# Attention outputs turned in 32x32 blocks on VectorE instead of whole on TensorE, in a decoder layer kernel

## Chip, cores and metric

The kernel runs on one core of a Trainium2 chip. The metric is the device time of one execution in microseconds (us). The kernel before takes 2980.4 us, the median of three runs (2975.87 to 2981.51).

## The reference

One decoder layer in float32 over `x` of 128 sequences x 128 tokens x 256: self attention, cross attention to `ctx` of the same shape, and a feed-forward part, each with layer norm ahead and a residual behind. 16 heads of 16 channels. Cut to what matters:

```python
def attn(xn, kv, mask):                     # self: kv = xn, no mask
    Q, K, V = proj(xn, Wq, bq), proj(kv, Wk, bk), proj(kv, Wv, bv)
    scores = einsum('bhqd,bhkd->bhqk', Q, K) / sqrt(16)
    if mask is not None:
        scores = where(mask == 0, 1e-9, scores)      # cross only
    out = einsum('bhqk,bhkd->bhqd', softmax(scores), V)
    return out.transpose(0, 2, 1, 3).reshape(B, S, 256) @ Wo.T + bo
x = x + attn(layernorm(x), layernorm(x), None)
x = x + attn(layernorm(x), ctx, mask)
x = x + ffn(layernorm(x))     # ternary weights, 256 -> 1024, gelu, layer norm, 1024 -> 256
```

Masked keys keep a weight of exp(1e-9 - max): they count in the softmax.

## The kernel before

There are three blocks of the program. `setup` turns and splits weights and builds masks, `attention` does both attentions, `ffn` the rest from a scratch tensor in HBM. The change is in `setup` (one constant) and `attention`.

`attention` works on groups of 4 sequences (G = 4, T = 512 tokens, 32 groups). Two chains of buffers exist, `self` and `cross`, each with four PSUM banks `self_bk`, `cross_bk`. The order is written out by hand, for each engine its own (`pe_slot`, `dve_slot`, `act_slot`, `pool_slot`, `sp_slot`), with semaphores between them. A `step` has two slots, and the engines run steps in a loop:

```python
        def step(slot, i):
            slot(crs, slf, present(i - 1), present(i), present(i + 1), present(i))
            slot(slf, crs, present(i + 1), present(i - 1), present(i), present(i + 2))
```

The arguments are y, x, att, tail, proj, norm. In a slot chain y does its attention core (scores, softmax, values of group att) while chain x ends another group (tail: divide, output projection), projects queries, keys and values of a third (proj), and y's next input is normalised (norm). The first slot, y = cross, is called the cross turn below, the second, y = self, the self turn. `proj` and `tail` work of x fills TensorE's time between scores.

The attention core. `pe_scores` (L802) computes scores of one sequence and eight heads, VectorE takes the maxima (`dve_max`, L651), TensorE waits for those of two steps before. The negated maxima are transposed by TensorE (L890), copied out by ScalarE (L604, `negmT`) and written by four DMAs into rows of `stk`. `pe_shifted` (L820) computes transposed, shifted scores; cross adds masks (L785). ScalarE exponentiates them (L630), and `pe_values` (L831) multiplies by the values, four heads into one bank of 128 partitions, 32 partitions (16 channels, a sum, padding) a head: four such sets, qd = 0 to 3, are called strips here. So the outputs have channels on partitions and queries on columns.

What happens to a strip: it is copied from PSUM into `oT`, a view of the `qk` buffer (VectorE L747 for qd 0 to 2, ScalarE L633 for qd 3); `pe_turn_outputs` (L838) turns it with four float32 transposes, so that queries lie on partitions; `dve_normalise` adds the masked sums in cross (L667), takes the reciprocal of the sums (L671) and multiplies (L673) into `att`. The last strip is handled at the head of the next slot, after the first maxima. `att` is split into two float16 parts (ScalarE L565, GpSimd L501), turned by TensorE (`turn_att`, L777), copied out by ScalarE (`both`, L549) into `ahl` and multiplied by the output weights (`products`, L766). ScalarE scales the product (L582), GpSimd adds the residual (L516), and in the cross turn VectorE normalises that for cross (`cross_xn`, L741).

The masked part of cross: `earg` from the negated maxima (L711), its exponential `ew` (L600), the sums of the masked values by TensorE (L949), both multiplied on VectorE into `ue` (L717, L720).

Queries and keys reach `stk` by DMA: SyncE issues 24 transfers a chain and group (`stack_rows`, L467) once ScalarE has written the four projection tiles (L540), the later ones also after VectorE's low parts (L644). The first scores of the chain wait for all 24.

Queue order that matters: ScalarE has `ew`, then `negmT`, then four DMA issues, then `products_out` (L582); GpSimd has the residual, its copy, `rstd` and the splits in that order; VectorE has `cross_xn` ahead of the strips of the cross turn.

## Time and profile before

| | |
|---|---|
| median of 3 runs | 2980.4 us |
| profiled execution, its own time | 2975.84 us |
| its span | 2973.8 us |
| granted TensorE clock, mean | 0.963 |
| busy: TensorE, VectorE, ScalarE, GpSimd | 2587.0, 2044.6, 1793.0, 977.4 us |
| attention loop | from about 88 to about 2330 us |

The page gives shares of the whole span, which has three stages with different limits. "Start" and "us" in a timeline are the start and length of a run of equal instructions; a bracket names the idle time before it on its engine and what ended it. PE is TensorE's matmuls, PEld its weight loads, DVE VectorE, ACT ScalarE, POOL GpSimd, SP SyncE. Float32 matmuls show as two records each.

### The profile page before, as it was taken

Reading aid. Unit: us, or ns where it says so; the run is one execution under the profiler, and the core shown is the slowest. Engines: PE = TensorE matmul, PEld = TensorE weight load, DVE = VectorE, ACT = ScalarE, POOL = GpSimd, SP = SyncE. Lnnn points to the kernel's source line nnn. Section 1 sums busy time; section 2 is a strip of 40 time slices with the busy share of each in tenths; the row PEclk is TensorE's granted clock in tenths of the full one; section 3 lists DMA queues with packets and bytes.
Section 4 is the critical chain, followed back from the end, with each engine's and each line's share of the span. In section 5 each row is a group of like instructions: output and inputs, shape, how many; then the busy total and the mean of one; then the engine's idle time right before and its main releaser. Section 6 shows DMA issues by size and latency. Waiting matters only on the chain. (4 is left out here: it accounts for less than half of the span.)

```text
span 2973.8 us, 79195 instructions
## 1 busy us (share of the span) xinstructions
PE 2587.0 (87%) x31607; PEld 1762.5 (59%) x31607; DVE 2044.6 (69%) x4066; ACT 1793.0 (60%) x2350; POOL 977.4 (33%) x630
## 2 busy tenths in 40 slices
PE   3478889898888998898998889998888499999999
PEld 2245556555555555555555555565555267777777
DVE  4256676776667666767766676667775288888887
ACT  1245665665665656656656656556665277777776
POOL 2223333333333333333333333333332133333432
PEclk7689999999999999999999999999999799999999
DMA  2133433333333334333333333333332211111111
GB/s 75 32 62 76 83 80 84 71 71 80 79 83 73 71 74 82 80 86 71 71 76 81 80 78 71 72 81 80 85 67 40 50 58 56 56 56 56 56 57 43
DMA packets 186380, 206.83 MB, mean 70 GB/s; under 512 B 35152, under 2 KB 136912, under 8 KB 186320
## 3 DMA queue, kind: packets, MB, share of 16 engines
q1 hardware_dynamic: 163056, 186.77, 27.0%
q10 hardware_dynamic: 23264, 19.22, 4.3%
q8 instruction: 43, 0.70, 0.1%
q14 instruction: 17, 0.14, 0.0%
HBM read 54.87 MB, written 33.55 MB: 30 GB/s over the span
## 5 line engine op out<-in xcount | busy, mean ns | idle before, releaser
L651 DVE TENSOR_REDUCE self_mx<-self_bk 128x8 f32<-128x1024 f32 x256 | 306.4, 1215 | 47.4 <-PE self_bk L802 47.2
L651 DVE TENSOR_REDUCE cross_mx<-cross_bk 128x8 f32<-128x1024 f32 x256 | 303.4, 1216 | 43.5 <-PE cross_bk L802 43.3
L630 ACT ACTIVATE prob<-cross_bk 128x1024 f32<-128x1024 f32 x256 | 248.3, 1022 | 75.6 <-PE cross_bk L820 75.2
L1244 PE MATMUL hbk<-wfcT,ffn_xhl 128*128 128x512 f16 x1024 | 263.8, 381 | 0.0
L1212 PE MATMUL ybk<-wpT,ghl 128*128 128x256 f16 x2048 | 260.2, 273 | 0.8 <-DVE ffn_y L1176 0.7
L630 ACT ACTIVATE prob<-self_bk 128x1024 f32<-128x1024 f32 x256 | 246.4, 1054 | 6.8 <-PE self_bk L820 6.6
L516 POOL TENSOR_TENSOR cross_src<-self_att,self_xb 128x1024 f32<-128x1024 f32 x32 | 75.4, 2356 | 532.6 <-ACT self_att L582 532.6
L1191 DVE SCALAR_TENSOR_TENSOR ghl<-tbk,lnwc,ghl 128x512 f16<-128x512 f32 x256 | 189.0, 739 | 73.7 <-ACT ghl L1120 72.0
L1212 PEld LDWEIGHTS ybk<-wpT,ghl 128*128 128x128 f16 x2048 | 200.1, 98 | 63.8 <-DVE ghl L1191 0.9
L1120 ACT ACTIVATE ghl<-tbk,lnwc 128x512 f16<-128x512 f32 x256 | 174.7, 683 | 75.4 <-PE tbk L1226 75.4
L747 DVE COPY self_qk<-cross_bk 128x512 f32<-128x512 f32 x96 | 66.4, 692 | 204.0 <-PE cross_bk L831 204.0
L1126 ACT ACTIVATE hid<-hbk 128x512 f32<-128x512 f32 x256 | 152.9, 597 | 64.1 <-PE hbk L1244 56.7
L758 PE MATMUL self_bk<-self_xhl,WT 128*128 128x512 f16 x768 | 188.8, 383 | 3.0 <-ACT self_xhl L549 2.0
L785 PE MATMUL cross_bk<-maskB,pick 64*128 64x512 bf16 x1024 | 158.0, 387 | 37.0 <-DMA cross_stk<-cross_qk 23.3
L497 POOL TENSOR_TENSOR self_rstd<-self_ve,mhalf 128x4 f32<-128x4 f32 x32 | 32.2, 1007 | 459.3 <-DVE self_ve L737 459.3
L1152 DVE BATCH_NORM_STATS2 hstats<-hid 128x6 f32<-128x512 f32 x256 | 173.9, 679 | 1.1 <-ACT hid L1126 0.8
L820 PE MATMUL self_bk<-self_stk 64*128 64x128 f16 x2048 | 96.9, 220 | 88.9 <-ACT prob L630 59.7
L785 PE MATMUL cross_bk<-maskBT,pick 64*128 64x512 bf16 x1024 | 157.0, 386 | 13.5 <-ACT prob L630 8.5
L540 ACT ACTIVATE self_qk<-self_bk,bcol 128x512 f16<-128x512 f32 x128 | 87.9, 686 | 126.6 <-PE self_bk L758 126.5
L1226 PE MATMUL tbk<-ident,hid 128*128 128x128 f32 x1024 | 153.5, 273 | 0.8 <-ACT hid L1126 0.8
L644 DVE SCALAR_TENSOR_TENSOR self_qk<-self_bk,bcol,self_qk 128x512 f16<-128x512 f32 x128 | 92.9, 745 | 85.9 <-ACT self_qk L540 85.9
L720 DVE TENSOR_TENSOR ue<-cross_bk,ew 128x512 f32<-128x512 f32 x64 | 44.3, 692 | 149.2 <-PE cross_bk L949 149.2
(200 smaller groups left out, 6068.7 us busy)
## 6 DMA issues: line engine op xcount, KB each, us to landing
self_stk<-self_qk SPq DMA_DIRECT2D x768, 64.0 KB, 2.3
cross_stk<-cross_qk SPq DMA_DIRECT2D x768, 64.0 KB, 2.3
self_src<-in_x SPq DMA_DIRECT2D x32, 512.0 KB, 3.9
ctx_in<-in_ctx SPq DMA_DIRECT2D x32, 512.0 KB, 4.8
x_scratch<-cross_att SPq DMA_DIRECT2D x32, 512.0 KB, 3.0
ffn_src<-x_scratch SPq DMA_DIRECT2D x32, 512.0 KB, 3.8
out<-ffn_y SPq DMA_DIRECT2D x32, 512.0 KB, 2.9
self_stk<-self_negmT ACTq DMA_DIRECT2D x128, 64.0 KB, 2.6
```

Source lines behind the costliest of these rows:

```text
L630: act.activation(y.prob[:, qd % 2, two:two + 2], y.bk[:, two:two + 2, :], ACT.Exp, scale=EXP_SCALE).then_inc(y.exp_done, 1)
L651: dve.tensor_reduce(ch.mx[:, 8 * m:8 * m + 8].rearrange("p (j r) -> p r j", r=2), ch.bk[:, o:o + 2, :].rearrange("p r (j k) -> p r j k", j ...
L758: last = nc.tensor.matmul(ch.bk[:, bank, :], sh.WT[:, w, wp, kt, tile * P:(tile + 1) * P], moving[:, a, kt, :], start=(n == 0 and kt == 0) ...
L785: pe.matmul(ch.bk[:, bank + r, :], sh.pick[rows, h], mask[rows, h], start=(h == 0), stop=False, skip_group_check=True)
L820: last = pe.matmul(ch.bk[:, bank + r, b * S:(b + 1) * S], ch.stk[rows, 1, p % 4, p // 4, b * S:(b + 1) * S], ch.stk[rows, 0, p % 4, p // 4 ...
L1120: act.activation(ghl[:, HI, s], tbk[:, TURN_BANK[s]], ACT.Copy, scale=sh.lnwc[:, s:s + 1]).then_inc(ghi_ready, 1)
L1126: act.activation(hid[:, half, s // 2, s % 2 * HF:(s % 2 + 1) * HF], hbk[:, s % 2], ACT.Gelu).then_inc(hid_ready, 1)
L1152: dve.bn_stats(hstats[:, s // 2, s % 2], hid[:, half, s // 2, s % 2 * HF:(s % 2 + 1) * HF]).then_inc(hstats_done, 1)
L1191: dve.scalar_tensor_tensor(ghl[:, LO, s], tbk[:, TURN_BANK[s]], sh.lnwc[:, s:s + 1], ghl[:, HI, s], ALU.mult, ALU.subtract).then_inc(glo_r ...
L1212: last = pe.matmul(ybk[:, b], ghl[:, part, t, b * S:(b + 1) * S], sh.wpT[:, t], start=(t == 0 and part == HI and b % 2 == 0), stop=(t == F ...
L1226: last = pe.transpose(tbk[:, TURN_BANK[s], b * S:(b + 1) * S], hid[:, 1 - half, b, s * P:(s + 1) * P], sh.ident[:, :])
L1244: last = pe.matmul(hbk[:, s % 2], xhl[:, half, part, kt, s // 2 * S:(s // 2 + 1) * S], sh.wfcT[:, kt, s % 2 * HF:(s % 2 + 1) * HF], start= ...
```

## The change

VectorE transposes each strip in 32x32 blocks, PSUM to PSUM, as soon as its values are there (`dve_turn_outputs`, all four strips). After that, partitions hold 32 queries of a block for each of four heads, columns hold block and channel. It divides in this layout, writes `att` so that two strips stand side by side in each 32 columns, and transposes `att` back in 32x32 blocks into `attT` (`dve_turn_att`, SBUF to SBUF, two halves): channels on partitions again, as the output projection needs them. ScalarE and GpSimd split `attT` into `ahl` directly. `pe_turn_outputs`, `turn_att`, the copies into `oT` and the copies into `ahl` are gone. The heads are dealt anew to strips (`stack_rows`, `pe_values`). The masked sums, their counts and exponentials are built in the same layout: 16 small matmuls turn the negated maxima (`m_turned`), L949 becomes 16 matmuls of 32 columns, and setup writes a count per block (`cntL`). In the core:

```diff
+        def dve_turn_outputs(dve, ch, g, qd):
+            dve.wait_ge(ch.pv_done, 4 * g + qd + 1)
+            dve.transpose(turned_bank(ch, qd), out_bank(ch, qd)).then_inc(ch.o_turned, 1)
         def dve_normalise(dve, ch, g, qd):
-            dve.wait_ge(ch.oT_ready, 4 * g + qd + 1)
-            o = turned_bank(ch, qd).rearrange("p (b h c) -> p b h c", b=G, h=4)[:, :, :, 0:HD + 1]
+            dve.wait_ge(ch.o_turned, 4 * g + qd + 1)
+            o = turned_bank(ch, qd).rearrange("p (b t c) -> p b t c", b=G, t=BLOCKS)[:, :, :, 0:HD + 1]
...
-                dve.tensor_tensor(total[:, qd], o, ue[:, :, 4 * qd:4 * qd + 4, :], ALU.add).then_inc(ch.den_ready, 1)
+                dve.tensor_tensor(o, o, ue[:, :, :, qd, :].rearrange("p t b c -> p b t c"), ALU.add).then_inc(ch.den_ready, 1)
...
+        def dve_turn_att(dve, ch, g, kt):
+            dve.wait_ge(ch.ao_ready, 4 * g + 2 * kt + 2)
+            wait(dve, ch.a_lo, 2 * (g - 1) + kt + 1)
+            dve.transpose(ch.attT[:, kt], ch.att[:, :, :].rearrange("p b d -> p (b d)")[:, kt * T:(kt + 1) * T]).then_inc(ch.aT_ready, 1)
...
+            if tail is not None:
+                dve_turn_outputs(dve, x, tail, QUADS - 1)
             maxima(0)
             if tail is not None:
                 dve_normalise(dve, x, tail, QUADS - 1)
+                dve_turn_att(dve, x, tail, 1)
             maxima(1, 2, 3)
...
-                    dve.wait_ge(y.negm_ready, att + 1)
-                    dve.tensor_scalar(earg[:, :], y.negm[:, :], 0.0, MASKED * HD ** 0.5, ALU.min, ALU.add).then_inc(earg_ready, 1)
+                    dve.wait_ge(m_turned, att + 1)
+                    dve.tensor_scalar(earg[:, :], y.bk[:, 1, 0:BLOCKS * G * QUADS], 0.0, MASKED * HD ** 0.5, ALU.min, ALU.add).then_inc(earg_ready, 1)
...
                 for qd in range(QUADS - 1):
-                    dve.wait_ge(y.pv_done, 4 * att + qd + 1)
-                    dve.tensor_copy(y.oT[:, qd], out_bank(y, qd)).then_inc(y.o_out, 1)
-                    if qd:
-                        dve_normalise(dve, y, att, qd - 1)
-                dve_normalise(dve, y, att, QUADS - 2)
+                    dve_turn_outputs(dve, y, att, qd)
+                    dve_normalise(dve, y, att, qd)
+                    if qd == 1:
+                        dve_turn_att(dve, y, att, 0)
...
-        def pe_turn_outputs(pe, ch, g, qd):
-            pe.wait_ge(ch.o_out, 4 * g + qd + 1)
-            for b in range(G):
-                last = pe.transpose(turned_bank(ch, qd)[:, b * S:(b + 1) * S], ch.oT[:, qd, b * S:(b + 1) * S], sh.ident[:, :])
-            last.then_inc(ch.oT_ready, 1)
...
-            def turn_att():
-                if tail is not None:
-                    pe.wait_ge(x.as_lo, 2 * tail + 2)
-                    turn_split(x, x.tb, x.asp).then_inc(x.aT_ready, 1)
...
+                    if y.cross:
+                        for jq in range(4):
+                            for block in range(BLOCKS):
+                                at = block * G * QUADS
+                                last = pe.matmul(y.bk[VW * jq:VW * (jq + 1), 1, at:at + G * QUADS], sh.ident16[:, VW * block:VW * (block + 1)],
+                                                 y.negm[:, :].rearrange("p (a j) -> p j a", j=4)[:, jq], start=True, stop=True, skip_group_check=True)
+                        last.then_inc(m_turned, 1)
...
-                for b in range(G):
-                    last = pe.matmul(y.bk[:, 2 + b // 2, (b % 2) * D:(b % 2 + 1) * D], sh.maskcT[:, :],
-                                     y.vals[:, b, :, 0:HD], start=True, stop=True)
-                    if b % 2:
+                for block in range(BLOCKS):
+                    for jq in range(4):
+                        heads = y.vals[:, :, :, 0:HD].rearrange("p b (k j s) d -> p j (b k) s d", k=KT, s=2)[:, jq]
+                        at = (block % 2) * D
+                        last = pe.matmul(y.bk[VW * jq:VW * (jq + 1), 2 + block // 2, at:at + D], sh.maskcT[:, VW * block:VW * (block + 1)],
+                                         heads, start=True, stop=True, skip_group_check=True)
+                    if block % 2:
                         last.then_inc(u_mm, 1)
+                pe.wait_ge(earg_ready, att + 1)
```

ScalarE's and GpSimd's side, and setup:

```diff
-            def split_outputs(ch, g, quads, cols):
+            def split_outputs(ch, g, kt):
                 if g is not None:
-                    act.wait_ge(ch.ao_ready, 4 * g + quads)
-                    act.activation(ch.asp[:, HI, :, cols], ch.att[:, :, cols], ACT.Copy).then_inc(ch.as_hi, 1)
+                    act.wait_ge(ch.aT_ready, 2 * g + kt + 1)
+                    act.activation(ch.ahl[:, HI, kt], ch.attT[:, kt], ACT.Copy).then_inc(ch.a_hi, 1)
...
-                both(x.aT_ready, x.ahl, x.tb, x.ahl_ready, tail)
...
-                act.wait_ge(y.pv_done, 4 * att + QUADS)
-                act.wait_ge(y.o_out, 4 * att + QUADS - 1)
-                act.activation(y.oT[:, QUADS - 1], out_bank(y, QUADS - 1), ACT.Copy).then_inc(y.o_out, 1)
...
+                for jq in range(4):
+                    for block in range(BLOCKS):
+                        nc.vector.tensor_scalar(cntL[VW * jq:VW * (jq + 1), block:block + 1], cntW[VW * block:VW * (block + 1), :], WS, None,
+                                                ALU.mult).then_inc(cnt_done, 1)
```

How rows move. First VectorE at the seam of a cross and a self turn, from the third strip of a cross group (names as in the text above; `cross_bk<-cross_bk` and `self_bk<-self_bk` with STREAM_TRANSPOSE are the turned strips). Before:

```order
L667 TENSOR_TENSOR total<-self_bk,ue 128x272 [waits cross_oT_ready]
L671 RECIPROCAL cross_rec<-total 128x16 [waits cross_den_ready]
L673 TENSOR_TENSOR cross_att<-total,cross_rec 128x4x64 [waits cross_rec_ready]
L651 TENSOR_REDUCE self_mx<-self_bk 128x2x4 [waits self_s_mm]
L667 TENSOR_TENSOR total<-cross_bk,ue 128x272 [waits cross_oT_ready]
L671 RECIPROCAL cross_rec<-total 128x16 [waits cross_den_ready]
L673 TENSOR_TENSOR cross_att<-total,cross_rec 128x4x64 [waits cross_rec_ready]
L651 TENSOR_REDUCE self_mx<-self_bk 128x2x4 [waits self_s_mm] x3
```

With the change:

```order
L682 STREAM_TRANSPOSE cross_attT<-cross_att 128x512 [waits cross_ao_ready]
L651 STREAM_TRANSPOSE self_bk<-self_bk 128x512 [waits cross_pv_done]
L666 TENSOR_TENSOR self_bk<-self_bk,ue 128x16x17 [waits cross_o_turned]
L670 RECIPROCAL cross_rec<-self_bk 128x16 [waits cross_den_ready]
L674 TENSOR_TENSOR cross_att<-self_bk,cross_rec 128x16x16 [waits cross_rec_ready]
L651 STREAM_TRANSPOSE cross_bk<-cross_bk 128x512 [waits cross_pv_done]
L644 TENSOR_REDUCE self_mx<-self_bk 128x2x4 [waits self_s_mm]
L666 TENSOR_TENSOR cross_bk<-cross_bk,ue 128x16x17 [waits cross_o_turned]
L670 RECIPROCAL cross_rec<-cross_bk 128x16 [waits cross_den_ready]
L674 TENSOR_TENSOR cross_att<-cross_bk,cross_rec 128x16x16 [waits cross_rec_ready]
L682 STREAM_TRANSPOSE cross_attT<-cross_att 128x512 [waits cross_ao_ready]
L644 TENSOR_REDUCE self_mx<-self_bk 128x2x4 [waits self_s_mm] x3
```

Four transposes stand in this stretch that did not: one ahead of the third strip's addition (a copy stood earlier), one ahead of the first maxima, and one each for the halves of `att`; the second one of these stands ahead of the second maxima.

TensorE at the same seam, from the last shifted scores of the cross turn. Before:

```order
L831 MATMUL self_bk<-prob,cross_vals 32x128 x16
L838 MATMUL self_bk<-ident,cross_qk 128x128 x4
L831 MATMUL cross_bk<-prob,cross_vals 32x128 x16
L838 MATMUL self_bk<-ident,cross_qk 128x128 x4
L802 MATMUL self_bk<-self_stk 128x128 x8
L838 MATMUL cross_bk<-ident,cross_qk 128x128 x4
L777 MATMUL cross_bk<-ident,cross_xs 128x128 x16
L802 MATMUL self_bk<-self_stk 128x128 x16
L777 MATMUL cross_bk<-ident,ctx_s 128x128 x16
L802 MATMUL self_bk<-self_stk 128x128 x8
```

With the change:

```order
L845 MATMUL self_bk<-prob,cross_vals 32x128 x16
L845 MATMUL cross_bk<-prob,cross_vals 32x128 x16
L816 MATMUL self_bk<-self_stk 128x128 x8
L791 MATMUL cross_bk<-ident,cross_xs 128x128 x16
L816 MATMUL self_bk<-self_stk 128x128 x16
L791 MATMUL cross_bk<-ident,ctx_s 128x128 x16
L816 MATMUL self_bk<-self_stk 128x128 x8
```

The three turns of strips are gone; the rest keeps its order.

TensorE in the cross turn, from the output products to the masked sums. Before:

```order
L766 MATMUL self_bk<-WT,self_ahl 128x256 x12
L890 MATMUL cross_bk<-ident,cross_negm 16x128 x4
L766 MATMUL self_bk<-WT,self_ahl 128x256 x12
L766 MATMUL self_bk<-WT,self_xhl 128x256 x24
L949 MATMUL cross_bk<-cross_vals,maskcT 128x256 x4
```

With the change:

```order
L780 MATMUL self_bk<-WT,self_ahl 128x256 x12
L893 MATMUL cross_bk<-ident,cross_negm 16x128 x4
L899 MATMUL cross_bk<-cross_negm,ident 32x16 x16
L780 MATMUL self_bk<-WT,self_ahl 128x256 x12
L780 MATMUL self_bk<-WT,self_xhl 128x256 x24
L957 MATMUL cross_bk<-cross_vals,maskcT 32x256 x16
```

Sixteen small matmuls are new behind the transposes of the negated maxima, and the masked sums are cut into sixteen.

## Rows read from the trace of the kernel before

**Rows 1.** The page's busy times, shares and instruction counts.
```profile
PE 2587.0 (87%) x31607; PEld 1762.5 (59%) x31607; DVE 2044.6 (69%) x4066; ACT 1793.0 (60%) x2350; POOL 977.4 (33%) x630
```

**Rows 2.** The tile maskcT: durations in ns, first and last start in us.
```profile
L949 PE MATMUL cross_bk<-cross_vals,maskcT x256: 379/379/634, 226.2 to 2332.2; 128*128 128x256 f32 x128
```

**Rows 3.** Timeline of VectorE: start us, length us, instruction, idle time before.
```profile
1126.43 1.27 DVE L747 COPY cross_qk<-self_bk 128x512 f32<-128x512 f32 x2
...
1130.93 0.43 DVE L667 TENSOR_TENSOR total<-self_bk,ue 128x272 f32<-128x272 f32 x1
1131.39 0.25 DVE L671 RECIPROCAL cross_rec<-total 128x16 f32<-128x16 f32 x1
1131.68 0.42 DVE L673 TENSOR_TENSOR cross_att<-total,cross_rec 128x256 f32<-128x256 f32 x1
...
1136.45 2.34 DVE L651 TENSOR_REDUCE self_mx<-self_bk 128x8 f32<-128x1024 f32 x2
...
1195.28 1.27 DVE L747 COPY cross_qk<-self_bk 128x512 f32<-128x512 f32 x2
```

**Rows 4.** Timeline of TensorE in the same group.
```profile
1127.17 0.66 PE L838 MATMUL self_bk<-ident,cross_qk 128*128 128x128 f32 x4 [1.67 <-DVE cross_qk L747]
...
1136.68 1.87 PE L777 MATMUL cross_bk<-ident,ctx_s 128*128 128x128 f16 x16 [1.43 <-DVE cross_att L673]
...
1139.02 1.95 PE L758 MATMUL cross_bk<-cross_xhl,WT 128*128 128x512 f16 x6
...
1145.58 1.47 PE L758 MATMUL cross_bk<-ctx_hl,WT 128*128 128x512 f16 x6
...
1165.26 0.61 PE L785 MATMUL cross_bk<-maskB,pick 64*128 64x512 bf16 x4 [0.29 <-DMA cross_stk<-cross_qk]
```

**Rows 5.** Timeline of TensorE in the next group.
```profile
1206.90 1.47 PE L758 MATMUL cross_bk<-cross_xhl,WT 128*128 128x512 f16 x6
...
1212.99 1.47 PE L758 MATMUL cross_bk<-ctx_hl,WT 128*128 128x512 f16 x6
```

**Rows 6.** Windows: busy us of each engine, PEclk, DMA share, GB/s.
```profile
1132.40:1136.60 4.20, 2.57 (x45) 2.00 (x44) 3.99 (x8) 2.84 (x4) 1.64 (x1) 1.00 0.00 0
1136.60:1139.00 2.40, 2.32 (x24) 1.98 (x24) 2.19 (x2) 0.80 (x2) 0.67 (x1) 0.50 0.00 0
```

**Rows 7.** Timeline of SyncE's queue: start, length of the issues.
```profile
1147.80 15.52 SPq L467 DMA_DIRECT2D cross_stk<-cross_qk  x24
...
1215.21 15.50 SPq L467 DMA_DIRECT2D cross_stk<-cross_qk  x24
...
1284.08 15.52 SPq L467 DMA_DIRECT2D cross_stk<-cross_qk  x24
```

**Rows 8.** Instructions grouped by line and shape: busy us, mean ns, idle before.
```profile
L831 PE MATMUL self_bk<-prob,cross_vals 128*32 128x128 f32 x3072 | 104.7, 277 | 0.0
L673 DVE TENSOR_TENSOR cross_att<-total,cross_rec 128x256 f32<-128x256 f32 x128 | 100.6, 786 | 4.4
L747 DVE COPY self_qk<-cross_bk 128x512 f32<-128x512 f32 x96 | 66.4, 692 | 204.0 <-PE cross_bk L831 204.0
L838 PE MATMUL self_bk<-ident,cross_qk 128*128 128x128 f32 x384 | 63.4, 288 | 52.9 <-DVE cross_qk L747 52.9
L949 PE MATMUL cross_bk<-cross_vals,maskcT 128*128 128x256 f32 x256 | 61.4, 383 | 0.0
L777 PE MATMUL cross_bk<-ident,cross_asp 128*128 128x128 f16 x512 | 35.0, 223 | 3.7 <-POOL cross_asp L501 3.7
L890 PE MATMUL cross_bk<-ident,cross_negm 128*16 128x128 f16 x128 | 12.5, 220 | 2.0 <-DVE cross_negm L709 2.0
```

**Rows 9.** Timeline of ScalarE in the cross turn.
```profile
1112.84 0.59 ACT L604 ACTIVATE cross_negmT<-cross_bk 16x512 f16<-16x512 f16 x1 [0.93 <-PE cross_bk L890]
...
1116.06 1.02 ACT L582 ACTIVATE self_att<-self_bk 128x1024 f32<-128x1024 f32 x1 [2.63 <-issue]
```

**Rows 10.** Timeline of VectorE in setup.
```profile
53.23 0.14 DVE L257 TENSOR_SCALAR cntW<-cntW 128x1 f32<-128x1 f32 x1
```

More of the change, by code:

```diff
@@ L31 @@
 VW = 32
+BLOCKS = S // VW
 WS = 8.0
@@ L77, in __init__ @@
         self.maskcT = sb("maskcT", [P, S])
-        self.cntW = sb("cntW", [P, 1])
+        self.cntL = sb("cntL", [P, BLOCKS])
         self.mfloor = sb("mfloor", [P, 1])
@@ L343, in __init__ @@
         self.prob = prob
-        self.oT = self.qk[:, :, :, :].rearrange("p a k t -> p (a k t)").bitcast(F32).rearrange("p (q t) -> p q t", q=QUADS)
         self.mx = sb(n + "_mx", [P, G * H])
@@ L350, in __init__ @@
         self.att = sb(n + "_att", [P, G, D])
-        self.asp = sb(n + "_asp", [P, 2, G, D], F16)
+        self.attT = sb(n + "_attT", [P, KT, T])
         self.ahl = sb(n + "_ahl", [P, 2, KT, T], F16)
@@ L381, in __init__ @@
         self.pv_done = sem(n + "_pv_done")
-        self.o_out = sem(n + "_o_out")
-        self.oT_ready = sem(n + "_oT_ready")
+        self.o_turned = sem(n + "_o_turned")
         if self.cross:
@@ L387, in __init__ @@
         self.ao_ready = sem(n + "_ao_ready")
-        self.as_hi = sem(n + "_as_hi")
-        self.as_lo = sem(n + "_as_lo")
         self.aT_ready = sem(n + "_aT_ready")
-        self.ahl_ready = sem(n + "_ahl_ready")
+        self.a_hi = sem(n + "_a_hi")
+        self.a_lo = sem(n + "_a_lo")
         self.op_mm = sem(n + "_op_mm")
@@ L416, in attention @@
         chl = sb("ctx_hl", [P, 2, KT, T], F16)
-        earg = sb("earg", [P, G * H])
-        ew = sb("ew", [P, G, H])
-        ue = sb("ue", [P, G, H, HD + 1])
-        total = sb("total", [P, QUADS, G, 4, HD + 1])
+        earg = sb("earg", [P, BLOCKS * G * QUADS])
+        ew = sb("ew", [P, BLOCKS, G, QUADS])
+        ue = sb("ue", [P, BLOCKS, G, QUADS, HD + 1])
         held = sb("held_wait", [P, 1])
@@ L449, in out_bank @@
         def out_bank(ch, qd):
-            return ch.bk[:, 2, :] if qd == QUADS - 1 else (slf if ch.cross else crs).bk[:, 2 + qd % 2, :]
+            return ch.bk[:, ch.tb, :] if qd == QUADS - 1 else (slf if ch.cross else crs).bk[:, 2 + qd % 2, :]
         def turned_bank(ch, qd):
-            return ch.bk[:, 1, :] if qd == QUADS - 1 else (slf if ch.cross else crs).bk[:, (0, 1, 3)[qd], :]
+            return ch.bk[:, ch.tb + 1, :] if qd == QUADS - 1 else (slf if ch.cross else crs).bk[:, (0, 1, 3)[qd], :]
         def stack_rows(sp, ch, g, block, heads):
@@ L465, in stack_rows @@
             for j in heads:
-                rows, to = slice(HD * j, HD * j + HD), HALF * (j % 2) + HD * block
-                sp.dma_start(ch.stk[to:to + HD, :, j // 2], ch.qk[rows, parts]).then_inc(ch.stacked, 16)
+                rows, to = slice(HD * j, HD * j + HD), HALF * (j // 2 % 2) + HD * block
+                sp.dma_start(ch.stk[to:to + HD, :, 2 * (j % 2) + j // 4], ch.qk[rows, parts]).then_inc(ch.stacked, 16)
         def sp_slot(sp, y, x, att, tail, proj, norm):
@@ L497, in deviations, with lo @@
                     nc.gpsimd.tensor_tensor(y.rstd[:, :], y.ve[:, :], sh.mhalf[:, :], ALU.pow).then_inc(y.rstd_ready, 1)
-            def lo(src, split, hi_ready, lo_ready, count, cols=slice(0, D)):
+            def lo(src, split, hi_ready, lo_ready, count):
                 pool.wait_ge(hi_ready, count)
-                nc.gpsimd.tensor_tensor(split[:, LO, :, cols], src[:, :, cols], split[:, HI, :, cols],
-                                        ALU.subtract).then_inc(lo_ready, 1)
+                nc.gpsimd.tensor_tensor(split[:, LO], src, split[:, HI], ALU.subtract).then_inc(lo_ready, 1)
             if tail is not None:
-                lo(x.att, x.asp, x.as_hi, x.as_lo, 2 * tail + 2, LAST)
+                lo(x.attT[:, 1], x.ahl[:, :, 1], x.a_hi, x.a_lo, 2 * tail + 2)
             if x.cross:
@@ L586, in act_slot @@
                 both(x.xT_ready, x.xhl, x.pb, x.xhl_ready, proj)
-                split_outputs(x, tail, 4, LAST)
+                split_outputs(x, tail, 1)
                 both(cT_ready, chl, x.tb, chl_ready, proj)
-                tiles(0, 1)
-                both(x.aT_ready, x.ahl, x.tb, x.ahl_ready, tail)
-                tiles(2, 3)
+                tiles(0, 1, 2, 3)
             else:
-                split_outputs(x, tail, 4, LAST)
+                split_outputs(x, tail, 1)
                 both(x.xT_ready, x.xhl, x.pb, x.xhl_ready, proj)
-                both(x.aT_ready, x.ahl, x.tb, x.ahl_ready, tail)
                 tiles(0, 1, 2, 3)
```

54 lines of the change are left out of this document (25 added, 29 removed).

## Prediction

> **What bounds the kernel now.** I read the page's busy shares first: TensorE is busy 87% of the span, VectorE 69% [rows 1]. Read alone, that says that matmul time removed is time gained. It is an average, so I took one group of the attention loop apart. The masked-sum matmuls of L949 come once a group, first at 226.2 and last at 2332.2 us [rows 2]: 31 distances of 67.9 us. A group has two halves: the cross turn (cross attention of one group beside the self projections) and the self turn (the reverse).
>
> In the timelines I looked for the wait that ends last in each half. Three pieces make up a group:
>
> *Piece 1, from the end of cross_xn on VectorE to the last projection tile of the self turn.* VectorE copies the first outputs from 1126.43, then adds, inverts and multiplies four strips while it also owes TensorE the first maxima; it hardly rests until 1138.8 [rows 3]. TensorE waits for it 1.67 us for a copy and 1.43 us for cross_att, then runs at half speed: the first tile takes 1.95 us instead of 1.47 in the next group [rows 4, 5]. The windows show the granted clock at 1.00 up to 1136.6 and 0.50 (1.2 GHz) after it; before the fall the engine had been busy 2.57 us of 4.2 [rows 6]. The last tile starts at 1145.58 and ends about 1.4 later, near 1147.0: piece 1 is 20.5 us. In the next group, at full clock, it is 19.1 (1195.28 to 1212.99 + 1.4) [rows 3, 5].
>
> *Piece 2, from that tile to the first cross scores.* SyncE issues 24 transfers of cross_qk in 15.5 us, from 1147.80, and the scores at 1165.26 end on one of them [rows 4, 7]. That is 18.2 us, whatever TensorE does meanwhile.
>
> *Piece 3, from those scores through projections, negated maxima, masked sums, residual and normalisation back to the end of cross_xn:* the rest, about 30.1 us, in which VectorE's maxima, TensorE and the ScalarE-GpSimd path of the residual take turns.
>
> The starts of the 24 transfers are 67.41 us apart around the full-clock group and 68.87 around another [rows 7].
>
> **The change part by part.**
>
> *Removed from TensorE.* Per group eight turns of four float32 transposes (L838): 63.4 us for 96 of them is 0.66 each, about 0.59 up to the next start, so 4.7 us; and two 16-transpose turns of the split outputs (L777), 35.0 us for 32, 1.09 each and about 0.9 net, so 1.8 us [rows 8]. ScalarE loses two wide copies and two narrow ones; neither piece 1 nor piece 2 waits for them, TensorE's tiles run meanwhile, so they count nothing (if it were short there, it would gain more). Three of the eight turns lie in piece 2: they count nothing, since the scores wait for the transfers. If the transfers were shorter, they would be worth 1.8 us.
>
> *Moved to VectorE.* In each half three copies (0.69 us, PSUM to SBUF) become 32x32 transposes, PSUM to PSUM, a fourth replaces ScalarE's copy, and two more turn the divided outputs. No 32x32 transpose is in the trace. From below I bound one by the 272-column addition, 0.43 us, from above by one maxima operation over 1024 columns, 1.17 (2.34 for two) [rows 3]. I take the copy's 0.69 [rows 8]: the same 512 columns and type, the same engine, a PSUM source. The Trainium skill has 311 ns for a transpose of 128 columns of bf16 (VectorE: DVE Perf Modes, The three transpose paths) and one element a cycle in that mode (Vector Engine (DVE) Microarchitecture Reference, 3.8); from these pages I estimate 0.71 us, which would move the sum by under 0.2 us a group, and no row here shows it.
>
> *Division.* The multiply in cross takes 0.79 us in the mean, but 0.42 where nothing disturbs it [rows 3, 8]. After the change its numerator comes from PSUM, as the self one's always does, and I take 0.42 for all.
>
> *Piece 1 after.* From the end of cross_xn VectorE is one chain. A strip is transpose 0.73 (0.69 and a semaphore), addition 0.46, reciprocal 0.29 and multiply 0.35 (0.42 less the overlap of an independent next one), by the distances in [rows 3]: 1.83. Two strips 3.7, turn of the first half 0.69, third strip 1.8: 6.2. Fourth transpose 0.6: 6.8. First maxima 1.15: 7.9. Addition, reciprocal, multiply of the fourth strip 1.2: 9.1. Turn 0.69: 9.8. Second maxima 1.15: 11.0. TensorE's fourth scores (0.3) and then the first tile wait for those second maxima, so the tile starts at 11.3; before it was 11.6 at full clock (1206.90 - 1195.28) [rows 3, 5]. The other tiles and scores need 6.6 us, 0.9 less than before, since the turn between them is gone. Piece 1 is 17.9: 1.2 saved. If the clock falls as before, the turn of ctx_s starts at 9.1 and takes 1.9, scores 0.6, the tile 1.95 [rows 4], the rest 5.2: 18.7, 1.8 saved against 20.5. So of the 3.3 us of turns and 3.1 us of waits that disappear from TensorE here, VectorE's chain hands most back: the wait for a copy becomes a wait for a transpose and a division.
>
> *Piece 3 after.* Gone are one L838 turn and the self turn of split outputs, 1.5 us. But VectorE now has the turn of the second half (0.69) ahead of the second maxima, and the next scores wait for those: walking it, the last self tile ends 0.3 us earlier than now. Then 16 small matmuls (32 weight columns, 16 moving columns) follow the negated maxima; the exponent's argument, ScalarE's exponential and, behind it, ScalarE's copy of the negated maxima wait for them. That copy (1112.84) stands ahead of four DMA issues, the output copy at 1116.06 [rows 9], GpSimd's residual and the next cross_xn: all of that moves. From below the matmuls cost 0.5 us together (L831: 104.7 us for 3072 halves, 0.03 each), from above 1.3 (L890: 12.5 us for 128, 0.10 less the overlap, 0.08 each) [rows 8]. I take 0.5, as these too write strips of 32; but four in a row write the same strip, which keeps the upper end open. With 0.25 for the argument, 0.1 net for the exponential ahead of the copy, and 0.3 off for the earlier tile, piece 3 grows by 0.55, at the upper end by 1.35. The masked sums become 16 matmuls to strips of 32 instead of 4 to 128 columns, now 61.4/32 = 1.9 us [rows 8]. L831 runs its four strips side by side (16 matmuls with 128 columns in 1.09, where four with 256 to full width need 1.9), so I leave them at 1.9; one after another they would be 7.
>
> *Sum.* Full-clock group: -1.2 + 0.55 = -0.65, 66.8. Low-clock group: -1.8 + 0.55 = -1.25, 67.6. The mean of 67.9 says that now about a third of the groups pay for the low clock. Afterwards TensorE waits four times 0.8 to 1.4 us around little work in piece 1, so I let two thirds pay: 67.3, or 0.65 to 0.7 less, times 31 = -21. The last group's turns, with no other work as cover, give 3 to 4 us. Setup, which everything waits for, has 15 more tiny VectorE operations like the one of 0.14 us [rows 10], half of it up to the next start: +1. In all -24. The profiled execution took 2975.8 (span 2973.8), so it would be 2952; the runs' median is 4.6 above it. Against that median: 2980.4 - 24 = 2956, its own range 2938 to 2974. A measurement of this kernel can tell about 0.2%, 6 us, from no change.
>
> TensorE's clock fell after a stretch in which transposes and waits alternated [rows 6]. The Trainium skill (TensorE: Matmul & The Clock Gate, PE-mode transpose) says that transposes don't count as activity like matmuls; by that rule taking them away can't bring the clock down, the share of low groups stays at a third, and the sum is -29, 2951.
>
> **The rivals.**
>
> *TensorE is the bound after all: 2788, chance 0.05.* 6.5 us less 0.5, times 32. For it: 87% busy. Against it: piece 2 ends on a transfer, piece 1 on VectorE.
>
> *Transposes are cheap: 2910, chance 0.10.* At 0.43 six of them on piece 1's chain save another 1.5 us a group: -46. For it: the engine does no arithmetic in them; against: nor does it in a copy.
>
> *Small matmuls one after another: 2980, chance 0.08.* 1.3 us instead of 0.5 is +0.8 a group, and the gain is gone.
>
> *The clock, slower: 3010, chance 0.12.* TensorE gets thinner exactly where it waits. If every group has a low stretch in piece 1 and a second one in piece 3 (where it will wait about 1 us just before the cross scores), each is 67.6 + 1.46 = 69.0: +1.1 x 31 = +33, less 3. It decides once every second group has the added stretch. For it: the clock fell after a 1.43 us wait. Against: it didn't after 1.67 us [rows 4, 6].
>
> *Transposes are dear: 3012 to 3056, chance 0.10.* At 1.0 us six on the chain cost 1.8 more a group, at 1.17 2.9; with piece 3's one or two +34 to +78 over no change. Gain and loss meet at about 0.80 us. Masked sums one strip after another would be worse still (+5 a group) and are in this chance.
>
> That the change doesn't do what it says is ruled out by the rows of the order: the turns are gone.
>
> **How the numbers follow.** Forecast 0.55, the rivals 0.05, 0.10, 0.08, 0.12, 0.10. The range 2908 to 3015 takes in cheap transposes, small matmuls and the clock; the first rival and most of the last, about 0.13, stay outside. Faster: the forecast less a margin, and 0.15: 0.68. Within 0.2%: 0.10. Slower: 0.22.
>
> **What would show it.** Right: 24 transfers again in 15.5 us and the cross scores ending on them, now after about 1 us of wait; VectorE without a gap from cross_xn to the third maxima, transposes at 0.65 to 0.75; TensorE's busy share down to some 81% with a span down by 1%; groups 67.3 apart. Wrong: cross scores that don't wait for a transfer, a transpose off 0.69 by over 0.1, small matmuls over 1 us, a clock below 1.00 in piece 3.

## The result, and the profile after

| | before | after |
|---|---|---|
| median | 2978.25 us (4 runs) | **3103.61 us** (4 runs, 3102.15 to 3113.85) |
| profiled execution / span | 2975.84 / 2973.8 us | 3104.04 / 3101.9 us |
| mean granted clock | 0.963 | 0.912 |

The ratio is 1.0428, 95% interval 1.0402 to 1.0453: 4.3% slower, where I forecast 0.8% faster (2956) and gave 3015 as the upper end. Ratios here and below leave out runs more than 1.5% above the fastest of their kernel; medians take in all of them. The page of the kernel after, busy times beside [rows 1], then its clock in 40 slices, then its instruction queue:

```profile
PE 2518.3 (81%) x30839; PEld 1644.6 (53%) x30839; DVE 2148.8 (69%) x4273; ACT 1636.0 (53%) x2222; POOL 975.3 (31%) x630
...
PEclk7689898899999899999999999999899889999999
...
q8 instruction: 285, 4.67, 0.6%
```

TensorE's busy time fell by 69 us, VectorE's rose by 104. The line that matters is the last: q8 moves instructions, in packets of 16 KB, and there are 285 of them. The page of the kernel before has 43:

```profile
q8 instruction: 43, 0.70, 0.1%
```

For the stretch from 400 to 2200 us, inside the attention loop, the views of the DMA queues say (packets, MB, share), first before, then after:

```profile
q8 instruction: 2, 0.03, 0.0%
```

```profile
q8 instruction: 222, 3.64, 0.9%
```

A group takes 72.8 us now, so this is 9 packets a group: the loop's instructions are fetched anew in every pass. The kernel before fetched none from 340.3 to 2189.0 us.

The sizes of single instructions held, but for the small matmuls, which took less. Instructions of the kernel after, grouped by line and shape (they answer to [rows 8]):

```profile
L651 DVE STREAM_TRANSPOSE cross_bk<-cross_bk 128x512 f32<-128x512 f32 x128 | 93.1, 727 | 147.4 <-PE cross_bk L845 147.4
L957 PE MATMUL cross_bk<-cross_vals,maskcT 128*32 128x256 f32 x1024 | 63.3, 389 | 0.0
L682 DVE STREAM_TRANSPOSE cross_attT<-cross_att 128x512 f32<-128x512 f32 x64 | 45.5, 711 | 7.9 <-DVE cross_att L674 0.2
L899 PE MATMUL cross_bk<-cross_negm,ident 128*32 128x16 f16 x512 | 9.5, 177 | 0.0
```

A 32x32 transpose of 512 columns takes 0.73 us (0.71 from SBUF) where I took 0.69; the masked sums take 63.3 us for 61.4; the 16 small matmuls 9.5/32 = 0.30 a group, for 0.5.

Where the time went, in one group. SyncE's queue, beside [rows 7]:

```profile
1061.84 18.34 SPq L469 DMA_DIRECT2D cross_stk<-cross_qk  x24
...
1135.39 17.37 SPq L469 DMA_DIRECT2D cross_stk<-cross_qk  x24
1152.98 1.32 SPq L488 DMA_DIRECT2D x_scratch<-cross_att  x1
...
1208.71 17.04 SPq L469 DMA_DIRECT2D cross_stk<-cross_qk  x24
```

TensorE, beside [rows 4]:

```profile
1150.78 1.08 PE L845 MATMUL self_bk<-prob,self_vals 128*32 128x128 f32 x32 [0.42 <-ACT prob L626]
1155.82 1.03 PE L799 MATMUL cross_bk<-maskB,pick 64*128 64x512 bf16 x4 [3.96 <-DMA cross_stk<-cross_qk]
```

The 24 issues take 17.0 to 18.3 us for 15.5, the scores come 20.4 us after the first of them for 17.5, after a wait of 3.96 us, and then TensorE runs at half clock: masks of 1.03 us for 0.61.

For the comparisons below I cut a group at four events: S1 from SyncE's first issue of cross_stk to the first cross scores, S2 to the masked sums, S3 to the end of cross_xn, S4 to the next first issue. (Piece 2 is S1 and the 0.8 us ahead of it, piece 3 is S2 and S3, piece 1 is S4 less 0.8.) Means over the middle 19 groups, us; "packets" is q8 of the whole run; "low" is the time at 1.2 GHz in one group, also a mean over these 19:

| kernel | median | S1 | S2 | S3 | S4 | group | packets | low |
|---|---|---|---|---|---|---|---|---|
| before | 2978.25 | 17.44 | 20.16 | 9.95 | 20.71 | 68.26 | 43 | 2.0 |
| after | 3103.61 | 20.24 | 21.05 | 10.49 | 20.99 | 72.76 | 285 | 12.4 |
| after_pad90 | 2997.60 | 17.47 | 20.31 | 10.29 | 21.06 | 69.14 | 43 | 6.8 |
| after_pad30 | 3128.08 | 20.12 | 22.79 | 10.29 | 20.58 | 73.78 | 285 | 14.2 |
| before_pad60 | 3098.24 | 20.71 | 21.59 | 9.94 | 20.57 | 72.81 | 286 | 6.1 |
| before_pad128 | 2976.60 | 17.44 | 20.16 | 9.94 | 20.72 | 68.26 | 44 | 2.0 |
| after_pad70_fill | 2946.56 | 17.48 | 20.39 | 10.29 | 19.23 | 67.39 | 43 | 0.5 |
| before_pad116_fill | 2948.02 | 17.46 | 20.16 | 9.95 | 19.85 | 67.42 | 44 | 0.0 |
| after_pad90_late | 2944.16 | 17.46 | 20.09 | 10.29 | 19.51 | 67.35 | 43 | 5.0 |
| after_pad90_twice | 3047.29 | 17.49 | 20.31 | 10.29 | 22.49 | 70.57 | 43 | 9.0 |
| after_late | 3062.71 | 20.65 | 21.23 | 10.57 | 19.03 | 71.48 | 285 | 10.6 |
| after_pad70_late_fill | **2914.49** | 17.39 | 20.09 | 10.29 | 18.46 | 66.23 | 43 | 0.4 |

### The profile page after: what moved, and what is told of

The parts are those of the page before. It is cut to its first block and busy times, and to the rows that moved or that the text cites. A ratio compares the mean times of both kernels' runs of the same rounds, so it can differ in the third digit from the quotient of the medians.

```text
span 3101.9 us, 77805 instructions
## 1 busy us (share of the span) xinstructions
PE 2518.3 (81%) x30839; PEld 1644.6 (53%) x30839; DVE 2148.8 (69%) x4273; ACT 1636.0 (53%) x2222; POOL 975.3 (31%) x630
## 5 line engine op out<-in xcount | busy, mean ns | idle before, releaser
L644 DVE TENSOR_REDUCE self_mx<-self_bk 128x8 f32<-128x1024 f32 x256 | 299.8, 1207 | 24.5 <-PE self_bk L816 23.7
L799 PE MATMUL cross_bk<-maskB,pick 64*128 64x512 bf16 x1024 | 193.3, 461 | 139.7 <-DMA cross_stk<-cross_qk 122.4
L816 PE MATMUL self_bk<-self_stk 48*128 48x128 f16 x2048 | 117.6, 244 | 108.0 <-DVE self_mx L644 50.6
L651 DVE STREAM_TRANSPOSE cross_bk<-cross_bk 128x512 f32<-128x512 f32 x128 | 93.1, 727 | 147.4 <-PE cross_bk L845 147.4
L564 ACT ACTIVATE self_ahl<-self_attT 128x512 f16<-128x512 f32 x64 | 42.5, 665 | 261.0 <-DVE self_attT L682 261.0
L816 PEld LDWEIGHTS self_bk<-self_stk 48*128 48x128 f16 x2048 | 67.1, 104 | 199.9 <-DVE self_mx L644 71.8
L539 ACT ACTIVATE cross_qk<-cross_bk,bcol 128x512 f16<-128x512 f32 x128 | 87.9, 687 | 159.5 <-PE cross_bk L772 159.5
```

The source lines that it names most:

```text
L539: act.activation(ch.qk[:, 1 + n // 2, n % 2], qk_bank(ch, n), ACT.Identity, bias=sh.bcol[:, 2 * ch.which + n // 2, n % 2:n % 2 + 1]).then_ ...
L644: dve.tensor_reduce(ch.mx[:, 8 * m:8 * m + 8].rearrange("p (j r) -> p r j", r=2), ch.bk[:, o:o + 2, :].rearrange("p r (j k) -> p r j k", j ...
L799: pe.matmul(ch.bk[:, bank + r, :], sh.pick[rows, h], mask[rows, h], start=(h == 0), stop=False, skip_group_check=True)
L816: last = pe.matmul(ch.bk[:, 2 * (m % 2) + r, j * S:(j + 1) * S], ch.stk[rows, 0, j, eight, b * S:(b + 1) * S], ch.stk[rows, 1, j, eight, b ...
```

## The experiments

Theory A: most of the loss is instruction loading, decided by where the loop's body happens to lie on the packets. Theory B, its rival: the chain of transposes on VectorE and the clock. For what A leaves over, two more: C, the clock, and D, VectorE's chain.

### Moving the loop by tiny matmuls

One edit in four doses: N matmuls of 16 columns, two instructions each, ahead of TensorE's attention loop. Nothing waits for them.

```diff
+                for _ in range(N):
+                    pe.matmul(slf.bk[:, 3, 0:16], sh.ident16[:, :], sh.ident16[:, 0:16], start=True, stop=True, skip_group_check=True)
                 steps(pe, pe_slot)
```

The changed kernel, N = 90:

> The changed kernel with 90 tiny matmuls (a weight load and a matmul each, 180 TensorE instructions, some 10 us in all at most) ahead of the attention's loop, nothing else changed. Theory A (TensorE's instructions are loaded anew in every group, because the loop's body now spans one 16 KB packet more than stays on the core): moved by 180 instructions the body spans one packet less, the packets of the instruction queue fall from some 9 a group to none during most of the loop, SyncE issues its 24 transfers in 15.5 us instead of 17.3, and the time falls by over 80 us, to 2940 to 3000 us. Rival B (the groups are longer because of the chain of transposes on VectorE and the clock that follows from it): 180 instructions ahead of the loop change nothing, 3100 to 3115 us, and the packets either stay or go without an effect.

**Measured: 2997.60 us**, ratio to before 1.0063 (1.0046 to 1.0080). 43 packets, none from 400 to 2200 us. SyncE issues in 15.5 us again, and TensorE waits about 1 us for the last transfer:

```profile
1093.23 15.52 SPq L469 DMA_DIRECT2D cross_stk<-cross_qk  x24
```

```profile
1110.71 0.61 PE L799 MATMUL cross_bk<-maskB,pick 64*128 64x512 bf16 x4 [1.03 <-DMA cross_stk<-cross_qk]
```

> A control for the run above: 30 tiny matmuls (60 TensorE instructions) ahead of the loop of the changed kernel. Theory A: by the count of instructions the body still spans the larger number of packets, so it stays at 3095 to 3115 us with some 9 packets a group. Rival B: 3100 to 3115 us as well. If this one is fast too, the place of packets isn't what I take it to be.

**Measured: 3128.08 us**, ratio 1.050 (1.0482 to 1.0517), 285 packets: loaded like N = 0, and 24 us slower than that, 13 us above the range that both theories had. It sits in S2 (22.79 for 21.05), with 7.8 us at low clock in it for 4.6; why the clock falls longer there stays open.

The kernel before, N = 60:

> The kernel before with 60 tiny matmuls (120 TensorE instructions) ahead of the loop. Theory A: the body of the kernel before then spans one packet more than it did, is loaded anew in every group (some 9 packets a group all along the loop, where it had none from 351 to 2200 us), SyncE's 24 transfers take 17 us and the time rises by 60 to 130 us, to 3040 to 3110 us. Rival B: only the matmuls' own time is added, 2978 to 2990 us.

**Measured: 3098.24 us**, ratio 1.0391 (1.0371 to 1.0411), 286 packets. The computation of the kernel before is untouched and it loses 120 us. Its SyncE and TensorE (S1 of one group):

```profile
1129.18 16.66 SPq L467 DMA_DIRECT2D cross_stk<-cross_qk  x24
```

```profile
1145.66 0.66 PE L838 MATMUL cross_bk<-ident,self_qk 128*128 128x128 f32 x4
1150.12 1.04 PE L785 MATMUL cross_bk<-maskB,pick 64*128 64x512 bf16 x4 [3.81 <-issue]
```

This is the picture of the kernel after: late issues, a long wait, half clock behind it. Here, though, the wait of 3.8 us ends on nothing that the profile shows: in this group the last transfer had landed 2.5 us before.

The late issues stand where instruction packets do. In the middle 19 groups of the kernel after, 22 issues are followed by the next only after 1.2 to 2.0 us instead of 0.6 or 0.7, and each of the 22 starts within 0.2 us of a packet's start. In before_pad60 there are 36, after 1.1 to 2.1 us, each within 0.6 us of a packet; in the kernel before and in after_pad90 there is none. Of the 2.8 us that S1 grows in the kernel after, 1.0 are these late issues. Another 1.4 come because the last transfer lands 3.7 us after its issue instead of 2.3, and 0.4 because TensorE starts 0.6 us after that instead of 0.2. How a packet holds up an issue or a transfer is not shown.

> The kernel before with 128 tiny matmuls (256 TensorE instructions, one packet's worth) ahead of the loop, so that the body lies on the packets as in the kernel before. Theory A: as the kernel before plus the matmuls' own time, 2978 to 2995 us, with no packets for most of the loop. Were the number of instructions in the whole program what decides, it would be as slow as the run with 120 more or slower.

**Measured: 2976.60 us**, ratio 1.0001 (0.9991 to 1.0011), 44 packets. 120 more instructions cost 120 us, 256 more cost nothing.

What follows. Theory B can't explain after_pad90 and before_pad60, where the time moves by 106 and 120 us together with the packets. For the two controls both theories forecast nearly the same time. A forecast the packets of all four runs and the time of those two; after_pad30 came out 13 us above A's range, before_pad128 1.4 us below it. It is the place that decides, not the number. Counted in TensorE's recorded instructions from the program's start, the bodies were at 3550 to 5293 (before, 1743 long) and 3389 to 5081 (after, 1692 long). Not loaded were bodies that began at 3550 or later and ended by 5293 (before_pad128 counted less one packet of 256; a later run adds one that began at 3538); loaded every time were those that began at 3389 and 3449, and one that ended at 5413. In the unrolled part a packet came for each 261 records ((5117 - 149)/19). So a body of some 1700 spans seven packets in a good place and eight in a bad one. The change took 161 instructions away ahead of the loop and 51 in it, and moved the beginning over a boundary.

The Trainium skill (Runtime: NRT & Kernel Launch, Instruction fetch mechanics) says that TensorE's instruction memory holds 128 KiB, 2048 instructions, filled in blocks of 256, and that a taken branch to something outside the window forces a fetch. The runs agree that a loop of 1743 instructions can stay and that the block is 256. Eight blocks would fit by the size too, yet such bodies are loaded whole. That the fetch of the next block ahead of the branch pushes out the first is my inference: 9 packets a group, one more than the eight, would fit it, but no run tests it. The same page's "2-page window", if it is meant for TensorE too, is contradicted: a seven-block body loaded nothing for 1849 us.

So 3103.6 - 2997.6 = 106 us of the result are loading. It sits in S1 (2.8 us a group), S2 (0.7), S3 (0.2). Part of it is the clock: in S2 TensorE is at 1.2 GHz for 4.6 us a group, without loading for none.

### What is left: the clock

Without loading the change still costs 20 us, where I forecast 24 less. S1 is as before, as forecast. S2 and S3 are 0.49 longer, for 0.55 forecast. S4 is 0.35 longer, for 1.2 to 1.8 shorter. Windows of after_pad90 in S4:

```profile
1077.70:1080.90 3.20, 0.74 (x17) 0.45 (x16) 3.13 (x6) 1.88 (x1) 1.15 (x1) 1.00 0.00 0
1080.90:1087.70 6.80, 6.03 (x43) 3.17 (x40) 4.76 (x6) 3.16 (x3) 1.15 (x1) 0.50 0.00 0
```

TensorE was busy 0.74 of 3.2 us, waiting for VectorE; then the clock is at 1.2 GHz for 6.8 us, in every one of the middle 19 groups. Before, the fall followed 2.57 busy us of 4.2 [rows 6] and lasted 3.4, in 11 of the 19:

```profile
1136.60:1140.00 3.40, 3.32 (x27) 2.40 (x28) 3.07 (x3) 1.80 (x2) 0.67 (x1) 0.50 0.00 0
```

TensorE in after_pad90, the head of the low stretch:

```profile
1081.70 1.89 PE L791 MATMUL cross_bk<-ident,ctx_s 128*128 128x128 f16 x16 [0.72 <-DVE cross_att L674]
1083.65 0.61 PE L816 MATMUL self_bk<-self_stk 48*128 48x128 f16 x8
1084.19 2.74 PE L772 MATMUL cross_bk<-cross_xhl,WT 128*128 128x512 f16 x6
```

The first tile takes 2.74 us, for 1.95 in [rows 4] and 1.47 at full clock. I filled TensorE's gaps with work of no use:

```diff
+            def fill(out, done, count, times):
+                pe.wait_ge(done, count)
+                for _ in range(times):
+                    pe.matmul(out, sh.ident16[:, :], sh.wfcT[:, 0, 0:512], start=True, stop=True, skip_group_check=True)
...
                     turn_input()
+                if tail is not None and att is not None:
+                    fill(slf.bk[:, 2, :], x.o_turned, 4 * tail + 3, 4)
                 scores(1)
+                if tail is not None:
+                    fill(x.bk[:, x.tb, :], x.o_turned, 4 * tail + 4, 5)
                 scores(2)
+                if tail is not None:
+                    fill(x.bk[:, x.tb, :], x.o_turned, 4 * tail + 4, 3)
```

> The changed kernel with 180 TensorE instructions ahead of the loop (2997.6 us), and 12 filler matmuls of 512 columns a group in the three gaps in which TensorE waits for VectorE after cross_xn; they write a bank that the next real matmul writes anew. Theory C (what is left of the loss is the clock: TensorE is at 1.2 GHz for 6.8 us in each group, in which the ctx turn and two projection tiles run): the low stretch shrinks or goes, the stretch from cross_xn to SyncE's transfers falls from 21.1 us towards 18.8, and the time to 2920 to 2960 us. Rival D (VectorE's chain of 32x32 transposes sets that stretch, clock or no clock): the clock rises and the time stays at 2985 to 3005 us.

**Measured: 2996.65 us** over 10 runs from 2956.55 to 3043.09, ratio 1.0017 (0.9983 to 1.0051). The median lies in D's range, but the groups are of two kinds: 16 of 31 are 67.3 us apart, at full clock, and 13 are 69.5 to 73.7, with 124 packets in the run. The body, 24 instructions longer, ended at 5309, at the edge of the eighth packet.

> The kernel before with 6 filler matmuls of 512 columns a group in the gap of 1.43 us ahead of the turn of ctx_s. In about two of three groups TensorE is at 1.2 GHz for 3.4 us there, which costs 1.5 us. Theory C: if the filler keeps the clock up in all of them, 20 x 1.5 = 30 us less, 2945 to 2960 us; if it keeps it in some, in between. Rival D: 2970 to 2985 us, no change.

Six fillers ahead of the turn of ctx_s alone. **Measured: 2999.05 us** (2963.54 to 3009.16), ratio 1.0054 (1.0024 to 1.0084): outside both ranges and no gain, for the same reason, 115 packets, the body ends at 5317. Both were inconclusive on the clock and told something on loading: at the edge it comes in some groups and not in others. Moved to a good place:

> As the run with 90 tiny matmuls and the filler, with 70 of them (40 instructions fewer ahead of the loop). That run had the clock up in nearly every group and groups 67.3 us apart in most, but some groups of 72.9 with instruction packets in them: its body, 24 instructions longer, ended at the edge of one more packet. Theory A with theory C: with 40 instructions fewer ahead no group loads, all are 67.3 apart and the time is 2930 to 2950 us, with a narrow spread. Rival (the filler itself disturbs some groups, by the clock or by PSUM): the spread and the median stay, 2955 to 3045 us.

**Measured: 2946.56 us** (2941.88 to 2948.64), ratio 0.9892 (0.9869 to 0.9915), 43 packets.

> The kernel before with its 6 filler matmuls a group (2999 us, with loading in about every third group) and 232 instructions ahead of the loop, nearly one packet, so that the longer body fits again. Theories A and C: all groups 67.4 us apart at full clock, 2945 to 2962 us. If the body doesn't fit there: 2980 to 3100 us, with packets in the loop.

**Measured: 2948.02 us**, ratio 0.9898 (0.9875 to 0.9920), 44 packets: less one packet of 256 its body lies at 3538 to 5293, and stays.

C holds: the filler gives the changed kernel 51 us and the one before 30, and S4 is 19.23 and 19.85 in nearly every group. And with loading and clock out of the way, the two kernels are **equal** within their spread, 2946.6 and 2948.0: VectorE's chain gives 0.6 us in S4 and piece 3 takes it back. (They carry 12 and 6 fillers a group, in different waits; no run has the same filler in both.) TensorE at full clock in the filled kernel:

```profile
1058.28 1.04 PE L906 MATMUL self_bk<-wfcT,ident 128*128 128x512 f16 x4
1059.51 0.40 PE L816 MATMUL self_bk<-self_stk 48*128 48x128 f16 x8 [0.20 <-DVE cross_att L674]
1060.15 1.25 PE L906 MATMUL cross_bk<-wfcT,ident 128*128 128x512 f16 x5 [0.24 <-DVE cross_bk L651]
...
1062.45 1.05 PE L791 MATMUL cross_bk<-ident,ctx_s 128*128 128x128 f16 x16
1064.30 0.40 PE L816 MATMUL self_bk<-self_stk 48*128 48x128 f16 x8 [0.80 <-DVE self_mx L644]
```

The turn of ctx_s takes 1.05 instead of 1.89, and TensorE waits again, 0.80 us, for the second maxima: behind the clock stands VectorE's chain.

### VectorE's chain

> The changed kernel with 180 TensorE instructions ahead of the loop (2997.6 us) and three more 32x32 transposes of 512 columns a group, ahead of those of the first three strips of the cross outputs, into a spare tile. Theory D: three times 0.65 to 0.72 us lie on VectorE's chain, 2.0 to 2.2 us a group more, 3055 to 3070 us. Theory C: TensorE's slow matmuls hide part of it, 3000 to 3050 us.

```diff
+            if ch.cross and qd < QUADS - 1:
+                dve.transpose(spare[:, qd], out_bank(ch, qd))
             dve.transpose(turned_bank(ch, qd), out_bank(ch, qd)).then_inc(ch.o_turned, 1)
```

**Measured: 3047.29 us**, ratio 1.0241 (1.0218 to 1.0264), 1.43 us a group in S4. Within C's range, under D's: in one group the three take 1.86 us up to the next start on VectorE, and a quarter of that doesn't reach the end of S4. With 9.0 us at low clock a group for 6.8, the clock's part isn't separated from the chain's here.

The other way, both turns of `att` off the chain (the first was in the slot before, behind the second strip; ScalarE's and GpSimd's splits move with them):

```diff
             if tail is not None:
                 dve_normalise(dve, x, tail, QUADS - 1)
+            maxima(1)
+            if tail is not None:
+                dve_turn_att(dve, x, tail, 0)
+            maxima(2)
+            if tail is not None:
                 dve_turn_att(dve, x, tail, 1)
-            maxima(1, 2, 3)
+            maxima(3)
...
-                    if qd == 1:
-                        dve_turn_att(dve, y, att, 0)
```

> The changed kernel with 180 TensorE instructions ahead of the loop (2997.6 us), the two turns of the divided outputs moved on VectorE behind the second and the third maxima of the next half, and ScalarE's and GpSimd's splits of them moved behind it too. They are 2 x 0.65 us of the chain from cross_xn to the second maxima, for which the first projection tile waits. Theory D (VectorE's chain sets the stretch): 1.3 us a group less in the cross half, some 0.6 in the self half where it bears, 2935 to 2960 us. Theory C (the clock alone): TensorE's gaps shrink a little, the clock may come back or not, 2960 to 3000 us.

**Measured: 2944.16 us**, ratio 0.9904 (0.9878 to 0.9930). S4 falls by 1.55, S2 by 0.22, 1.8 us a group, where D had 1.3 and 0.6. The time is in D's range, but not all of it is the chain: low clock also falls, from 6.8 to 5.0 us a group, and between the two filled kernels of the table the same move takes S4 only from 19.23 to 18.46. So about half of the 1.55 is the chain and the rest comes with the clock. VectorE of this kernel:

```profile
1056.26 0.42 DVE L674 TENSOR_TENSOR cross_att<-cross_bk,cross_rec 128x256 f32<-128x256 f32 x1
1056.60 1.21 DVE L644 TENSOR_REDUCE self_mx<-self_bk 128x8 f32<-128x1024 f32 x1
1057.73 0.70 DVE L682 STREAM_TRANSPOSE cross_attT<-cross_att 128x512 f32<-128x512 f32 x1
1058.36 1.19 DVE L644 TENSOR_REDUCE self_mx<-self_bk 128x8 f32<-128x1024 f32 x1
1059.47 0.69 DVE L682 STREAM_TRANSPOSE cross_attT<-cross_att 128x512 f32<-128x512 f32 x1
```

The second maxima follow the division at once; the turns go between maxima, where TensorE is in its tiles. The same program without the instructions ahead:

> The version with the late turns without any instructions put ahead of the loop, so that TensorE's body lies as in the changed kernel. Theory A: it is loaded in every group, some 285 instruction packets, 3035 to 3070 us, about 100 above the 2944.2 of the same program with 180 instructions more. Rival (what matters is the order on VectorE alone): 2940 to 2950 us.

**Measured: 3062.71 us**, ratio 1.0288 (1.0266 to 1.0311), 285 packets. The version that is 1% faster than the kernel before with 180 instructions ahead is 2.9% slower without them, and q8 tells why. With everything together:

> The version with the late turns (2944.2 us) with the filler in the three gaps of TensorE after cross_xn, 140 instructions ahead of the loop. Theory C: low clock still takes 5 us a group there; with it gone the stretch from cross_xn to SyncE's transfers falls from 19.5 to about 18.0 us, 31 x 1.4 = 45 us less, 2895 to 2920 us. Theory D alone (VectorE's chain, no worth in the clock): 2935 to 2950 us.

**Measured: 2914.49 us** (2911.63 to 2915.50), ratio 0.9787 (0.9766 to 0.9809): the fastest, 2.1% under the kernel before. S4 went from 19.51 to 18.46, where C had 18.0; two of the 19 groups still have a low stretch.

## Why the prediction was wrong

- **The step that failed** is in *piece 2*: "That is 18.2 us, whatever TensorE does meanwhile", and with it the 15.5 us for 24 issues, taken as fixed. They are fixed only while no instructions are loaded. The rows to see that were there: in the trace of before, SyncE's first sets, while packets still came, took longer than the 15.5 of [rows 7]:

```profile
185.89 17.28 SPq L467 DMA_DIRECT2D cross_stk<-cross_qk  x24
221.47 16.82 SPq L467 DMA_DIRECT2D self_stk<-self_qk  x24
...
259.75 16.28 SPq L467 DMA_DIRECT2D cross_stk<-cross_qk  x24
```

  Loading is worth 106 of the 148 us between forecast and result: 2.8 us a group in piece 2, 0.9 in piece 3. No rival of mine had it. Once placed well, piece 2 was right: 17.47 us for 17.44, the scores ending on the transfer after 1.03 us of wait, as "what would show it" said.
- **The clock** was the right mechanism, too small. I let two thirds of the groups pay 0.8 us over a full-clock group. Without loading all pay, and the low stretch lasts 6.8 us, not 3.4: 69.1 for 67.3 at full clock, 1.8. I had also misread the kernel before: "now about a third of the groups pay for the low clock" came from the mean of 67.9, and this holds the shorter groups of the loop's end. In its middle 19 groups 11 pay, 1.5 us each, and the mean is 68.26. The rival "the clock, slower" (3010, chance 0.12) put its second low stretch into piece 3; there it came only with loading. Without loading the second half of the low stretch follows the first, in piece 1. Its 3010 is the nearest to the 2997.6 of that run, but by chance: its second low stretch wasn't there. I had applied the remark of the Trainium skill on transposes and clock (TensorE: Matmul & The Clock Gate, PE-mode transpose) as "taking them away can't bring the clock down". That did not hold here: 2.0 us of low clock a group became 6.8. What lowers it, the turns that are gone or the waits that are new, no run separates.
- **Piece 1's chain** was 0.5 too short: the first maxima start 7.28 us after cross_xn instead of 6.8, because the first two strips take 2.1 each for 1.83. VectorE of the kernel after, from the end of cross_xn:

```profile
1188.01 0.72 DVE L651 STREAM_TRANSPOSE self_bk<-self_bk 128x512 f32<-128x512 f32 x1
1188.96 0.45 DVE L666 TENSOR_TENSOR self_bk<-self_bk,ue 128x272 f32<-128x272 f32 x1 [0.23 <-DVE self_bk L651]
...
1190.08 0.72 DVE L651 STREAM_TRANSPOSE self_bk<-self_bk 128x512 f32<-128x512 f32 x1
...
1195.29 1.18 DVE L644 TENSOR_REDUCE self_mx<-self_bk 128x8 f32<-128x1024 f32 x1
```

  At full clock (after_pad70_fill) the first tile starts at 11.8 for 11.3, S4 saves 0.6 for 1.2.
- **Piece 3** was right in its sum, 0.49 for 0.55, in part by luck. Means over the 19 groups of after_pad90 beside those of before: ScalarE's copy of the negated maxima starts 0.48 us later behind their turn, for 0.85 in my terms (the small matmuls took 0.30 for 0.5). But that turn, counted from the first cross scores, comes only 0.07 us earlier, for 0.3. The two errors nearly cancel, and cross_xn ends 0.50 us later. Transposes (0.73 for 0.69) and masked sums (1.98 for 1.9 a group) were right in kind; so the rivals "dear transposes", "cheap transposes" and "small matmuls one after another" are out. "TensorE is the bound" is out too: after_pad90 has 129 us less of TensorE's busy time than before and is 20 us slower.
- The full-clock group, forecast at 66.8, is 67.4 in after_pad70_fill: 0.6 of mis-sized chain. The 3 to 4 us for the last group and the 1 us of setup were not measured apart.

## What to carry to other kernels

Before you explain a loop's time after any edit, count the packets of the instruction queue inside it: if there were none and now there are, part of what you measure is where the loop lies. For the changed kernel 140 to 180 idle instructions ahead of it gave that back; fewer instructions in it should do the same, but that wasn't tried. Compare two versions only at the same state of loading and clock; here this turned +4.3% into zero. And when work moves off TensorE to an engine that TensorE then waits for, price the clock of what follows the wait, and look whether the moved work can stand behind what is waited for.
